# The second expert layer of a graph and mixture-of-experts kernel: 36 blocks on two tables become 30 on one

## The reference

```python
logits = flat @ router_w.T                      # 1354 tokens x 128, 8 experts
probs = jax.nn.softmax(logits, axis=-1)
topk_probs, topk_idx = jax.lax.top_k(probs, 2)
topk_probs = topk_probs / (jnp.sum(topk_probs, axis=-1, keepdims=True) + 1e-09)
gates = jnp.einsum('nk,nke->ne', topk_probs, jax.nn.one_hot(topk_idx, 8))
h = jax.nn.silu(jnp.einsum('nc,ehc->neh', flat, w1)) * jnp.einsum('nc,ehc->neh', flat, w3)   # hidden 341
y = jnp.einsum('neh,ech->nec', h, w2)
out = jnp.einsum('ne,nec->nc', gates, y)
```

## Time and profile before

| | us |
|---|---|
| three runs | 529.75, 531.85, 537.24 |
| median | 531.85 |
| span of the profiled execution | 520.2 |
| median less span | 11.65 |
| PE busy in the span | 450.7 |
| DVE busy in the span | 342.4 |

### The profile page before, as it was taken

How to read it: one execution, slowest core, us unless ns; L and a number is a source line. 1 busy time by engine, 2 the same in 40 slices (tenths; PEclk the granted TensorE clock), 3 DMA queues, 4 the chain that set the end, 5 groups by cost and what they waited for, 6 DMA issues and landing times.

```text
span 520.2 us, 6589 instructions
## 1 busy us (share of the span) xinstructions
PE 450.7 (87%) x1892; PEld 268.2 (52%) x1892; DVE 342.4 (66%) x753; ACT 239.3 (46%) x390; POOL 69.8 (13%) x115
## 2 busy tenths in 40 slices
PE   4588598977698998998979999999988878999996
PEld 2533454544355664454644444444444556787875
DVE  0997979787648772225773887787577655744572
ACT  4987789577777552104134031222213036644441
POOL 5000000000011000000000000100600502564442
PEclk9679788989989999999999999999989999999999
DMA  8889500000000000000000000530100111122422
GB/s 282 275 265 372 238 0 0 0 1 1 0 2 1 0 2 0 1 0 3 1 0 0 1 0 31 184 111 20 45 6 1 48 43 44 53 68 64 123 68 84
DMA packets 27006, 31.70 MB, mean 61 GB/s; under 512 B 3490, under 2 KB 20591, under 8 KB 26967
## 3 DMA queue, kind: packets, MB, share of 16 engines
q1 hardware_dynamic: 25111, 27.71, 16.8%
q0 software_dynamic: 1856, 3.51, 2.0%
HBM read 19.44 MB, written 11.77 MB: 60 GB/s over the span
## 4 chain that ended last, share of the span: by engine, by line
PE 53%; DVE 25%; ACT 11%; issue 9%; POOL 1%; DVEq 0%; POOLq 0%; ACTq 0%
PE bank L1340 9%; PE bank L1149 4%; PE bank L1422 4%; PE bank L1406 4%; PE bank L1288 4%; PE bank L1407 3%; DVE pr_ring L2074 3%; PE bank L1110 2%; DVE y_units L1551 2%; PE bank L1329 2%; DVE y_units L1562 2%; PE bank L999 2%; PE bank L1413 2%; DVE hr_ring L1877 2%; DVE t_units L1557 2%
## 5 line engine op out<-in xcount | busy, mean ns | idle before, releaser
L1340 PE MATMUL bank<-pr_ring,hW 128*128 128x512 f32 (+3 forms) x198 | 94.1, 560 | 6.1 <-DVE pr_ring L2074 5.4
L2074 DVE SCALAR_TENSOR_TENSOR pr_ring<-adjT,regR,bank 128x512 f32<-128x512 f32 (+3 forms) x99 | 64.7, 680 | 35.5 <-PE bank L1329 34.0
L1340 PEld LDWEIGHTS bank<-pr_ring,hW 128*128 128x128 f32 (+1 forms) x198 | 34.4, 193 | 35.3 <-DVE pr_ring L2074 18.4
L999 PE MATMUL bank<-y_units,msg 128*128 128x512 f32 (+3 forms) x66 | 34.4, 652 | 15.1 <-DVE y_units L1572 15.0
L1110 PE MATMUL bank<-hr_ring,W2s 128*128 128x512 f32 (+1 forms) x96 | 45.3, 560 | 0.0
L1877 DVE TENSOR_TENSOR hr_ring<-hr_ring,bank 128x512 f32<-128x512 f32 (+1 forms) x48 | 29.5, 619 | 20.9 <-ACT hr_ring L796 14.9
L585 POOL DMA_INDIRECT yg<-pr_ring,goes x32 | 31.2, 976 | 50.9 <-DVE pr_ring L2113 49.0
L796 ACT ACTIVATE hr_ring<-bank,b1c 128x512 f32<-128x512 f32 (+1 forms) x48 | 29.8, 628 | 15.7 <-PE bank L972 15.7
L970 PE MATMUL bank<-zhi,W1hi 128*128 128x512 f32 (+1 forms) x48 | 35.1, 731 | 0.3 <-DVE zlo L1546 0.3
L2125 DVE TENSOR_TENSOR hbuf<-hbuf,bank 128x341 f32<-128x341 f32 x36 | 18.3, 508 | 23.9 <-PE bank L1407 21.1
L579 POOL DMA_INDIRECT xg<-rowx,slot x22 | 22.3, 1013 | 69.6 <-DVE slot L1684 63.5
(11 more groups left out here) (321 smaller groups left out, 889.9 us busy)
## 6 DMA issues: line engine op xcount, KB each, us to landing
xg<-zeros SPq DMA_DIRECT2D x1, 3575.0 KB
xg<-zeros SPq DMA_DIRECT2D x1, 3055.0 KB
wall<-in_w SPq DMA_DIRECT2D x2, 1364.0 KB
adjT<-in_adjT SPq DMA_DIRECT2D x1, 2560.0 KB
xblk<-xg SPq DMA_DIRECT2D x36, 65.0 KB
adjT<-in_adjT SPq DMA_DIRECT2D x1, 1650.0 KB
adjT<-in_adjT SPq DMA_DIRECT2D x3, 512.0 KB, 5.9
adjT<-in_adjT SPq DMA_DIRECT2D x1, 1024.0 KB
```

The lines of the kernel that those rows point to most:

```text
L999: mm = nc.tensor.matmul(B_GNN[:, 0:w], msg[0:r, j, :], y_units[0:r, g % RINGY, i, 0:w], start=(j == 0), stop=(j == T - 1))
L1340: nc.tensor.matmul(B_ACC[:, 0:w], hW[0:r, j, k * P:(k + 1) * P], ring[0:r, 0:w], start=(k == 0 and j == 0), stop=(k == K - 1 and j == T - ...
L2074: nc.vector.scalar_tensor_tensor(out=pr_ring[0:r, 4 + p % R_RING, 0:w], in0=adjT[0:r, j, cols(c)], scalar=g_col[0:r, j, k:k + 1], in1=B_F[ ...
```

## The change

There is one table `xg` and one `yg`. A region of an expert holds all its rows of all tiles. The groups are now tiles 0 to 7 (positions of chunks 0 and 1) and tiles 8 to 10. Of the rows that tiles 0 to 7 leave, 15 early blocks are made: first all full blocks, then one more for the experts with the fullest rest, until there are 15. The 15 late blocks begin at each expert's first row that no early block holds and run through the rows of tiles 8 to 10. So the early blocks wait for the sends of tiles 0 to 7, and the sends of tiles 8 to 10 wait until all early blocks are loaded, because an early block may read past the rows then written. The last seven blocks are joined on chip, for the three tiles 8 to 10 alone. Sums of tiles 0 to 7 go to POOL and their store to ACT; sums of tiles 8 to 10 to DVE, in the last iteration.

```diff
-GROUPS = [(0, 6), (6, T)]
-BLOCKS = [(2 * (min(N, b * P) - a * P) + E * (P - 1)) // P for a, b in GROUPS]
+GROUPS = [(0, 8), (8, T)]
+EARLY = 15
+LATE = 15
+BLOCKS = [EARLY, LATE]
+DEEP = 4
-YRING = 6
+YRING = 8
+OWN = 8
+NEW = T - OWN
-         9: [("starts", 1)], 10: [("list", 1)]}
-DVE1B.setdefault(FETCH - AHEAD + 3, []).append(("combine",))
+         9: [("order",)], 10: [("list", 1)]}
-KEEP = 4
+KEEP = LATE - E
+DVE1B.setdefault(5, []).append(("spans",))
+DVE1B.setdefault(NB - 1, []).append(("combine",))
...
             for b in range(NB):
                 block_load(b)
-                if b == FETCH:
-                    for i in range(YRING):
-                        sp.wait_ge(s[f"y_out{i}"], 16 * len(range(i, BLOCKS[0], YRING)))
-                    for j in range(2):
-                        sp.dma_start(*fetched(0, j)).then_inc(s["got0"], 16)
+            for i in range(AHEAD):
+                sp.wait_ge(s[f"y_out{i}"], 16 * len(range(i, NB - KEEP, AHEAD)))
+            for j in range(2):
+                sp.dma_start(*fetched(1, j)).then_inc(s["got1"], 16)
+            for j in range(2):
+                sp.dma_start(*fetched(0, j)).then_inc(s["got0"], 16)
...
             def send(t, j):
...
+                if t == OWN and j == 0:
+                    for i in range(AHEAD):
+                        pool.wait_ge(s[f"xb_in{i}"], 16 * len(range(i, EARLY, AHEAD)))
+                    pool.wait_ge(s["sent0"], 32 * OWN)
+                    pool.iota(rowx[:, 0:NEW, :, P:P + 1].rearrange("p t j o -> p t (j o)"), pattern=[[P, NEW], [IDS, 2]], base=FIRST + OWN * P,
+                              channel_multiplier=1, allow_small_or_imprecise_dtypes=True).then_inc(s["tables_const"], 1)
+                    pool.wait_ge(s["tables_const"], CONSTS1 + 1)
...
             def block_sent(b):
+                at(pool, f"y_out{b % AHEAD}", 16 * (b // AHEAD))
                 pool.wait_ge(s["y_set"], b + 1)
...
-            a, b = GROUPS[1]
-            pool.wait_ge(s["xtok_set"], C)
-            pool.wait_ge(s["got0"], 64)
-            pool.tensor_tensor(answer[:, a:b, :], x3tok[:, a:b, :], picked_y[:, 0, a:b, :], ALU.add).then_inc(s["summed"], 1)
+            pool.wait_ge(s["xtok_set"], 2)
+            pool.wait_ge(s["got0"], 32)
+            pool.tensor_tensor(answer[:, 0:OWN, :], x3tok[:, 0:OWN, :], picked_y[:, 0, 0:OWN, :], ALU.add).then_inc(s["summed"], 1)
...
                 hidden_turned(NB - 1)
+                act.wait_ge(s["summed"], 2)
+                act.dma_start(out_d[0:OWN * P, :].rearrange("(t p) d -> p t d", p=P), answer[:, 0:OWN, :]).then_inc(s["out_done"], 16)
...
-                for t in range(*GROUPS[1]):
-                    i = t - GROUPS[1][0]
-                    mm = nc.tensor.matmul(joined_tile(t), joiner[:, k, i * P:(i + 1) * P], yblk[:, b % YRING, :], start=(k == 0 and i in (0, 4)), stop=(k == KEEP - 1 and i >= 3))
+                for i in range(NEW):
+                    mm = nc.tensor.matmul(B_SIDE[:, i * P:(i + 1) * P], joiner[:, k, i * P:(i + 1) * P], yblk[:, b % YRING, :],
+                                          start=(k == 0 and i == 0), stop=(k == KEEP - 1 and i == NEW - 1))
...
                     if b > 1:
                         down(b - 2, bases.pop(b - 2))
+                    if b - 3 >= NB - KEEP:
+                        join(b - 3)
```

More of the change, by code:

```diff
@@ L1381, in prefix @@
                 for i, t in enumerate(own):
-                    r, first = rows(t), GROUPS[group(t)][0]
-                    mm = nc.tensor.matmul(B_SIDE[:, i * E:(i + 1) * E], before[0:r, :], mk[0:r, t, :], start=True, stop=(t == first))
-                    for q in range(first, t):
+                    mm = nc.tensor.matmul(B_SIDE[:, i * E:(i + 1) * E], before[0:rows(t), :], mk[0:rows(t), t, :], start=True, stop=(i == 0))
+                    for q in own[:i]:
                         mm = nc.tensor.matmul(B_SIDE[:, i * E:(i + 1) * E], oneb[:, 0:1].to_broadcast([P, P]), mk[:, q, :], start=False, stop=(q == t - 1))
-                for g, a, b in runs(c):
-                    first, end = GROUPS[g]
-                    if b == end:
-                        for q in range(first, end):
-                            r = rows(q)
-                            mm = nc.tensor.matmul(B_SIDE[:, n * E:(n + 1) * E], oneb[0:r, 0:1].to_broadcast([r, P]), mk[0:r, q, :],
-                                                  start=(q == first), stop=(q == end - 1))
+                for i, t in enumerate(own):
+                    r = rows(t)
+                    mm = nc.tensor.matmul(B_SIDE[:, n * E:(n + 1) * E], oneb[0:r, 0:1].to_broadcast([r, P]), mk[0:r, t, :], start=(i == 0), stop=(i == n - 1))
                 mm.then_inc(s["pos_ps"], 1)
@@ L1684, in route_slots @@
                 nc.vector.tensor_copy(slot[:, a:b, :], red1[:, 0:k, :]).then_inc(s["slot_set"], 1)
-            def route_starts(g):
-                share, start, end = (shares1[0:1, i, :] for i in range(3))
-                link(nc.vector.tensor_scalar(share, share, ROUND, ROUND, ALU.add, ALU.subtract))
-                square = cmp[0:1, 0:E, :]
-                link(nc.vector.tensor_tensor(square, tri[0:1, :, :], share.unsqueeze(1).to_broadcast([1, E, E]), ALU.mult))
-                link(nc.vector.tensor_reduce(start, square, AX.X, ALU.add))
-                link(nc.vector.tensor_tensor(end, start, share, ALU.add))
@@ L1695, in route_list @@
-            def route_list(g):
-                share, start, end = (shares1[0:1, i, :] for i in range(3))
-                nb, first = BLOCKS[g], sum(BLOCKS[:g])
-                done = cmp[0:1, 0:nb, :]
-                link(nc.vector.tensor_tensor(done, end.unsqueeze(1).to_broadcast([1, nb, E]),
-                                             bno[0:1, 0, 0:nb].unsqueeze(2).to_broadcast([1, nb, E]), ALU.is_le))
-                expert, row = place1[0:1, 0, 0:nb], place1[0:1, 1, 0:nb]
+            turn_no, held, full, key, share1, opens, closes, spans, left = (counts1[0:1, i, :] for i in range(9))
@@ L2109, in block_out @@
                 at(dve, "y_ps", b + 1)
[L2110 removed]
+                at(dve, f"y_out{b % AHEAD}", 16 * (b // AHEAD - 1))
                 if b < NB - KEEP:
```

188 lines of the change are left out of this document (114 added, 74 removed).

## The result

The kernel after takes 523.13 us (median of four, 522.2 to 527.13), the kernel before 531.28 us beside it: a ratio of 0.9843, 95% interval 0.9806 to 0.9879, so -8.3 us (-10.3 to -6.4). Timed once more against before, it gave 0.9864 (0.9817 to 0.9911). The forecast was -2.6 us; the gain is about three times that, and 523.13 lies just above the lower end of the range.

The account below looks back on a forecast made before the run. The chain of waits was taken as bound, TensorE holding half and VectorE a quarter, with late blocks TensorE-bound. Terms -13.56 + 4.3 + 0.75 + 4.6 + 0.25 - 0.3 + 1.4 gave -2.6: 531.85 to 529.3 us, range 523 to 535.

Parts of the forecast that it names:

- Six blocks less: Late, TensorE-bound part of the expert stage: 30 blocks in place of 36, 2.26 us each, -13.56 us.
- The first block starts later: Start of the expert stage: block 0's load waits for 16 sends in place of 12, +4.3 us (3.9 to 5.3).
- first wait covered: Rival, first blocks: the chain of tiles 8 to 10 sets the pace up to block 7; 523.6 us, chance 0.17.
- The clock: TensorE behind block 0: idle time brings the lower clock level, +1.4 us, bounds 0 and 3.4 for both waits.
- DVE's 13 steps: Attention loop: the early-block list takes 13 small VectorE steps in place of 4, +1.9 us, hidden by the later load.
- the spans: Behind VectorE's output of block 3: five more small steps ahead of the routing, +0.75 us (0.3 to 1.1).
- The 18 steps of order and list: VectorE ahead of block 15: 18 steps in place of 11, about 5.9 us against 2.5, costed at nothing inside the wait.
- A new wait for block 15: Before block 15: sends of tiles 8 to 10 start later and its load waits for them, +4.6 us (3.5 to 6.8).
- which I leave as it is: Whole kernel: the median of the runs lies 11.65 us above the profiled span; the forecast kept that gap unchanged.
- Joins and sums: Last blocks: seven joins take 42 matmuls in place of 40, +0.25 us; first tiles' sums leave VectorE, -0.3 us.
- they come out at nothing: End of the kernel: VectorE's sums of tiles 8 to 10 fall where TensorE ends and were costed at nothing.
- tail: Rival, end of the kernel: fetches or GpSimd's sums come after TensorE's end, 3 us late; 532.3 us, chance 0.08.

Follow-up runs that it names:

- before_wait: The kernel before, with block 0's load also waiting for the sends of tiles 6 and 7; 537.35 us, ratio 1.0111 against before.
- after_again: The kernel after, unchanged, timed again beside the version with earlier VectorE sums and later GpSimd sums; 527.04 us, ratio 0.9864 against before.
- before_short: The kernel before with 11 late blocks in place of 17, the six blocks' rows not computed; 521.64 us, ratio 0.9805 against before.
- before_block15: The kernel before; sends of tiles 8 to 10 wait until 15 blocks are loaded, block 15's load waits for these sends; 532.2 us, ratio 1.0011.
- before_again: The kernel before, unchanged, timed and profiled once more; 532.56 us, ratio 1.0018 against before.
- before_send512: The kernel before with the sends of tiles 8 to 10 cut to rows of 512 bytes in place of 520; 530.58 us, ratio 0.9961.
- after_port: The kernel after, VectorE's sums of tiles 8 to 10 one block earlier, GpSimd's sums waiting for VectorE's last placement mask; 525.79 us, ratio 0.9843 against before.
- after_port_again: The same kernel as after_port, timed once more beside the kernel after; 521.69 us, ratio 0.9799 against before.

## Why the prediction was wrong

**Six blocks less: right.** 2.26 us each before and after; the stretch from block 16 to the last block is 43.19 - 31.25 = 11.94 us shorter, with three joins in it.

**The first block starts later: right in place and near in size.** Load 0 at 417.86 (417.9), transposes at 419.81 (420.0) and 420.94 (421.25). Alone, in before_wait, it costs 5.9 us (3.2 to 8.6) with its clock, predicted 5.7. The measured 523.13 us lies by the 523.6 of the rival "first wait covered", but by luck: its condition does not hold. By the table the means of the eight traces of the after kind and of the seven of before without before_wait and the profiled one are 423.2 and 420.3 at block 0, and 32.6 and 31.6 from there to block 10: +3.9 us.

**The clock: right in kind, in place only in half of the traces.** The low clock lies behind block 0 in before_wait and in four of the eight traces of the after kind, such as after_again (0.80 from 420 to 425), where the step from block 0 to block 1 is 4.2 us in place of 2.54; but in before_short, which has no such wait, it does so too (4.22 us). In after it lies in the loop (0.66 from 410 to 415), behind a stretch in which PE was busy for 0.59 of 2 us (407 to 409). So the term was some 1.7 us or nothing, within the bounds 0 and 3.4. The Trainium skill (TensorE: Matmul & The Clock Gate, Part 1: The HAM clock gate) says that an idle PE falls to the lower level; these stretches agree, as the earlier trace rows did.

**DVE's 13 steps and the spans: right.** Load 0 stands behind the sends, not behind the list. The spans show in the step from block 6 to block 7: 6.07 us in after (438.47 to 444.54), 5.75 before, so +0.3, the lower bound. The 18 steps of order and list add up to some 5.3 us from the prediction's own step times, not 5.9; as they were put at nothing, the sum does not change by it.

**A new wait for block 15, +4.6 us: this is the step that failed.** By itself it measured +0.6 us (-1.2 to 2.4). PE does wait for block 15's load, 3.54 us in before_block15 and 4.91 in after_again; in after it does not. What failed is that the wait was added to a PE that otherwise keeps its pace there. The way from block 10 to 16 takes 22.5 us on average in the six traces of after with these sends in a row, and 22.5 in the four of before and its variants that send in a row without a wait (before_again, before_wait, before_short, before_send512). The price was set against an execution in which that way took 14.75. The 11.65 us between the span and the median, "which I leave as it is", were 1.8 us of remainder and, for the most part, a stall of some 8 to 9 us that the profiled execution did not have: the six sends held up PE. (In before_again 8.66 us are lost there and 1.71 ahead of block 0.) A wait that falls on such a stall adds little. It may not be nothing: the three of those six traces of after in which PE waits for the load (after_again, after_port, after_port_again) take 23.3 us on average, the other three 21.6. No rival had this wait alone covered; the forecast without its 4.6 us is -7.2.

**Joins and sums: too low.** Each join between blocks takes its 0.67 us (2.93 from block to block in place of 2.26), where before had all four behind the last block; the 0.25 us counted only the matmuls more. The ends of before and of after_port differ by 13.24 - 12.65 = 0.6 us in favour of after, so of the three joins' 2.0 us some 1.4 remain, less the 0.3 for the sums that left.

**VectorE's sums, "they come out at nothing": wrong.** VectorE's sums at the end lay under GpSimd's and held up the last blocks, 14.73 us to the end in place of 12.65: +1.6 to 2.1 us. This was the mechanism of the rival "tail", 0.08, in another form: not GpSimd's sums were late, VectorE waited for them. The Trainium skill (SBUF — State Buffer, Who interferes with whom) says that VectorE and GpSimd share one pair of ports under an exclusive lock, and that a VectorE instruction with two inputs from SBUF contends with a GpSimd one that reads SBUF. The traces agree: L2157, which has two such inputs, takes 2.24 us in place of 0.16 and ends with GpSimd's sum.

**The sum, from the table's means.** +3.9 (start and clock) + 0 (block 15) - 11.9 (late blocks, with joins) + 1.2 (end: 14.5 - 13.24) = -6.8 us; the two series gave -8.3 and -7.3. Against the forecast it is 2.5 us less at the start with the spans, 4.6 less at block 15, and 2.9 more in the late blocks and the end. The table has one trace for each run. By the times, the three single changes add up to 5.9 + 0.6 - 10.4 = -3.9 us; their intervals are some 2 to 3 us wide to either side, and before_short's end (16.34 us) is longer than after's, so the parts are not known to better than a few us.

**What stays open.** Why the profiled execution of before escaped the stall, alone of all that are known of that kernel. Nor is it known by what way the indirect sends delay PE: its matmuls are recorded at their usual pace while those who wait for them are released 4 to 5 us late. The sends alone don't explain it either: the last eight sends in the attention loop, of the same kind and 1.26 us apart (405.68 to 414.52 in after), show no such late release in any trace. Whether the recording of the trace takes part can't be told from here, as no execution without it is known.

## What to carry over

Where the profiled span and the timed runs differ by more than a steady remainder, the profile lacks something that the runs have: find its place first, since a wait that the change puts there may cost next to nothing. Price a wait against what the place already loses, not against a clean stretch. Before two engines sum side by side, look whether their operands all lie in SBUF.

## What the runs showed of the hardware

- Among the first blocks, six indirect transfers of up to 128 rows, one every 1.3 to 1.7 us, cost the kernel before 8 to 9 us, in which the engines that wait for TensorE were released late; eight like them in the attention loop, 1.26 us apart, showed no such release. The same rows as plain transfers cost nothing of it (14.75 us from block 10 to 16), cutting the rows to 512 bytes changed little (-2.1 us), and one indirect transfer with each block's output (one per 2.26 us, late blocks) left PE at its full pace. The Trainium skill (SBUF — State Buffer, Who interferes with whom) says that a DMA never contends with a compute engine; here the measurement says that something of these transfers does reach TensorE, whatever the way.
- While GpSimd runs a sum of 1024 elements per partition (2.35 us), a VectorE instruction on two operands of one element per partition, both in SBUF, takes 2.24 us in place of 0.16, and a scaled mask of 384 elements from SBUF 2.58 in place of 0.42 beside the next such sum; instructions that read PSUM take their usual 0.35 to 0.51 us.
